# Leaving part of the scores uncopied and moving the side work of two interleaved attention loops

## Time and profile before

| | |
|---|---|
| median of 3 runs | 2729.12 us (2728.18 to 2730.86) |
| the profiled execution, its own time | 2727.77 us |
| its span | 2726.0 us |
| busy share of the span: PE, DVE, ACT, POOL | 85%, 92%, 94%, 47% |
| mean granted clock of PE | 0.979 |
| DMA | 140.84 MB, mean 52 GB/s |

### The profile page before, as it was taken

The page is one execution under the profiler, slowest core; times in us unless marked ns, Lnnn a source line. Parts: engine busy times, 40 slices in busy tenths (PEclk is TensorE's granted clock), DMA queues, the critical chain, the costliest instruction groups (busy, mean ns, idle before and its releaser), DMA issues. The chain is left out here.

```text
span 2726.0 us, 39855 instructions
## 1 busy us (share of the span) xinstructions
PE 2310.4 (85%) x12453; PEld 1084.6 (40%) x12672; DVE 2501.0 (92%) x3626; ACT 2558.9 (94%) x4763; POOL 1279.9 (47%) x1891
## 2 busy tenths in 40 slices
PE   5788888877777777777778899999999999999998
PEld 2244444433433433443342334343433434333434
DVE  5899999999999999999988999999999999999995
ACT  4899999999999999999998999999999999999994
POOL 0146566654554554554552244444344444434444
PEclk8799999999999999999999999999999999999999
DMA  7511212133211111111111111111011111111110
GB/s 212 124 55 50 82 52 72 49 93 87 64 35 43 33 35 40 38 35 35 51 33 41 49 43 35 41 45 46 29 47 44 36 39 45 43 31 47 44 30 16
DMA packets 190938, 140.84 MB, mean 52 GB/s; under 512 B 92163, under 2 KB 177669, under 8 KB 190726
## 3 DMA queue, kind: packets, MB, share of 16 engines
q1 hardware_dynamic: 190406, 137.69, 18.4%
q10 hardware_dynamic: 320, 0.59, 0.1%
HBM read 92.04 MB, written 41.94 MB: 49 GB/s over the span
## 5 line engine op out<-in xcount | busy, mean ns | idle before, releaser
L1059 DVE TENSOR_REDUCE nmax<-score 128x1 f32<-128x1024 f32 x1024 | 1196.7, 1212 | 105.7 <-PE score L823 98.8
L1032 DVE TENSOR_SCALAR_CACHE_REDUCE big<-score 128x1024 f32<-128x1024 f32 x1024 | 1194.7, 1217 | 48.2 <-PE score L761 45.5
L1264 ACT ACTIVATE big<-big,nmax 128x1024 f32<-128x1024 f32 x1024 | 1168.1, 1143 | 36.8 <-DVE big L1032 33.1
L1306 ACT ACTIVATE score<-score,nmax 128x1024 f32<-128x1024 f32 x1024 | 1119.8, 1100 | 45.7 <-DVE nmax L1059 44.5
L823 PE MATMUL score<-big,shared 128*128 128x512 bf16 x1956 | 619.7, 397 | 271.3 <-ACT score L1306 236.4
L761 PE MATMUL score<-shared 128*128 128x512 bf16 x1921 | 534.6, 382 | 57.5 <-DVE big L1032 40.3
L742 PE MATMUL bank_g<-big,qw 128*32 128x512 f32 x4096 | 492.6, 599 | 1.0 <-ACT qcol L1291 1.0
L823 PEld LDWEIGHTS score<-big,shared 128*128 128x128 bf16 x2048 | 130.2, 98 | 566.1 <-ACT score L1306 474.0
L761 PEld LDWEIGHTS score<-shared 128*128 128x128 bf16 x2048 | 165.3, 98 | 429.1 <-DVE big L1032 253.9
L717 PE MATMUL bank_f<-norms,w_fc_sb 128*128 128x128 f32 x2048 | 297.1, 278 | 45.5 <-ACT hid L1228 44.5
L717 PEld LDWEIGHTS bank_f<-norms,w_fc_sb 128*128 128x128 f32 x2048 | 278.5, 192 | 114.0 <-ACT hid L1228 75.3
(11 more groups left out here) (147 smaller groups left out, 1747.5 us busy)
## 6 DMA issues: line engine op xcount, KB each, us to landing
shared<-q_parts SPq DMA_DIRECT2D x256, 64.0 KB, 2.4
shared<-kb_parts SPq DMA_DIRECT2D x256, 64.0 KB, 2.2
shared<-vb_parts SPq DMA_DIRECT2D x256, 64.0 KB, 2.2
big<-k_parts SPq DMA_DIRECT2D x48, 192.0 KB, 5.1
big<-k_parts SPq DMA_DIRECT2D x24, 256.0 KB, 7.9
kb_parts<-pieces SPq DMA_DIRECT2D x96, 64.0 KB, 1.6
vb_parts<-pieces SPq DMA_DIRECT2D x96, 64.0 KB, 1.6
shared<-in_x SPq DMA_DIRECT2D x32, 128.0 KB, 2.3
```

Source lines behind the costliest of these rows:

```text
L1032: v.tensor_scalar(row_chunk(c), score_b(turn, c)[:, :], -1.0, INF, ALU.mult, ALU.min, accum_out=nmax[:, par, c // NCH, c % NCH:c % NCH + 1 ...
L1059: v.tensor_reduce(nmax[:, par, c // NCH, c % NCH:c % NCH + 1], score_a(turn, c)[:, :], AX.X, ALU.max, negate=True).then_inc(max_a, 1)
L1264: a.activation(row_chunk(c), row_chunk(c), ACT.Exp, bias=nmax[:, par, c // NCH, c % NCH:c % NCH + 1], scale=-1.0, accum_out=esum[:, par, c ...
L1306: a.activation(s[:, :], s[:, :], ACT.Exp, bias=nmax[:, par, c // NCH, c % NCH:c % NCH + 1], accum_out=esum[:, par, c // NCH, c % NCH:c % N ...
```

## The change

Three things are changed together.

1. In the second attention the slots in `STAGED` (21 of 32) keep the copy. In the other 11 (0, 4, 5, 7, 13, 14, 15, 26, 29, 30, 31) DVE does a reduction, as in the first attention, and ACT takes the exponential from PSUM into SBUF. For these the bank is free when the exponential is done.
2. The slots of the side work of the second attention: up projections, relu, down projections, y, the first list of `PROD_AT`, the copy of the product (slot 17 to 16), the copy of the transposed input (24 to 27), and DVE's statistics and mean (24, 25 to 27, 28).
3. In the first attention the slot numbers become a table. `BESIDE` has the old numbers and is used for iterations 0 to 10 and from 31 on; `ALONE` has new ones for iterations 11 to 30. The copy of q is split between slots 19 and 30 there.

```
+BESIDE = dict(turn_opt=9, out=[10, 11], turn_x2=12, kv=[13, 14, 15, 16], q=[18, 20],
+              turn_x1=17, up=[18, 19, 20, 21, 22, 23, 24, 25], down=[26, 26, 27, 27, 28, 29, 30, 30],
+              fac=1, take_opt=7, take_x2=10, take_x1=15, take_k=15, take_v=15,
+              take_q=[20, 20], relu=[19, 23], take_y=29,
+              rec=4, add=11, stats_x1=12, mean_x1=13, stats_x2=6, mean_x2=7)
+ALONE = dict(turn_opt=7, out=[8, 9], turn_x2=10, kv=[12, 13, 15, 15], q=[17, 19],
+             turn_x1=18, up=[19, 21, 21, 21, 23, 23, 24, 24], down=[26, 26, 27, 28, 29, 30, 31, 31],
+             fac=0, take_opt=5, take_x2=9, take_x1=17, take_k=14, take_v=14,
+             take_q=[19, 30], relu=[20, 23], take_y=30,
+             rec=3, add=9, stats_x1=14, mean_x1=15, stats_x2=1, mean_x2=5)
+UP_B = [0, 0, 1, 1, 3, 5, 5, 5]
+DOWN_B = [14, 16, 17, 17, 18, 18, 20, 21]
+RELU_B, TAKE_Y_B, KEEP_B = [0, 5], 20, 16
+STAGED = [1, 2, 3, 6, 8, 9, 10, 11, 12, 16, 17, 18, 19, 20, 21, 22, 23, 24, 25, 27, 28]
+TURN_B, COLUMNS_B = 24, 27
-PROD_AT = [7, 7, 10, 10, 13, 13, 16, 16], [22, 22, 25, 25, 28, 28, 31, 31]
+PROD_AT = [6, 6, 9, 9, 12, 12, 15, 15], [22, 22, 25, 25, 28, 28, 31, 31]
...
+        def plan(it):
+            return ALONE if N_STEPS <= it < T - 1 else BESIDE
...
-                need(pe, max_b, CPT * i + c - NBUF + 1)
+                need(pe, max_b if (c - NBUF) % CPT in STAGED else exp_b, CPT * i + c - NBUF + 1)
...
-                v.tensor_scalar(row_chunk(c), score_b(turn, c)[:, :], -1.0, INF, ALU.mult, ALU.min,
-                                accum_out=nmax[:, par, c // NCH, c % NCH:c % NCH + 1]).then_inc(max_b, 1)
+                if c in STAGED:
+                    v.tensor_scalar(row_chunk(c), score_b(turn, c)[:, :], -1.0, INF, ALU.mult, ALU.min,
+                                    accum_out=nmax[:, par, c // NCH, c % NCH:c % NCH + 1]).then_inc(max_b, 1)
+                else:
+                    v.tensor_reduce(nmax[:, par, c // NCH, c % NCH:c % NCH + 1], score_b(turn, c)[:, :],
+                                    AX.X, ALU.max, negate=True).then_inc(max_b, 1)
...
-                        if c == 24:
+                        if c == 27:
                             ffn_stats_of(T + i1, (quad + 3) % 4, x3_ready, i1 + 1)
-                        if c == 25:
+                        if c == 28:
                             ffn_mean(T + i1)
...
-                a.activation(row_chunk(c), row_chunk(c), ACT.Exp, bias=nmax[:, par, c // NCH, c % NCH:c % NCH + 1], scale=-1.0,
+                staged = c in STAGED
+                a.activation(row_chunk(c), row_chunk(c) if staged else score_b(turn, c)[:, :], ACT.Exp,
+                             bias=nmax[:, par, c // NCH, c % NCH:c % NCH + 1], scale=-1.0 if staged else 1.0,
                              accum_out=esum[:, par, c // NCH, c % NCH:c % NCH + 1]).then_inc(exp_b, 1)
```

More of the change, by code:

```diff
@@ L841, in phase_a @@
                             transpose2(bank_f, opt).then_inc(opt_tr, 1)
[L842 to L849, removed]
+                        for k in range(KC):
+                            if c == at["out"][k]:
+                                if k == 0:
+                                    pe.wait_ge(opt_T, i1 + 1)
+                                mm(bank_f[:, D:2 * D], optT[:, k, :], w_out_sb[:, k, :], start=(k == 0), stop=False)
+                                if k == KC - 1:
+                                    mm(bank_f[:, D:2 * D], ones[:, :], bias[:, D:2 * D], start=False, stop=True).then_inc(oproj, 1)
+                        if c == at["turn_x1"]:
                             ffn_transpose(i1, xn)
                         for f in range(FF // P):
-                            if c == UP_A[f]:
+                            if c == at["up"][f]:
                                 ffn_up(i1, f)
                         for f in range(FF // P):
-                            if c == DOWN_A[f]:
+                            if c == at["down"][f]:
                                 ffn_down(i1, f)
@@ L1039, in head_maxima, with out_stats @@
                     row_min(i, par, 1)
-            def out_stats(i3, r, c):
-                if c == 6:
+            def out_stats(i3, r, c, at):
+                if c == at["stats_x2"]:
                     dve.wait_ge(ffn_out, i3 + 1)
                     v.bn_stats(st[:, 1, :], xout[:, r, :]).then_inc(qkv_stats, 1)
-                if c == 7:
+                if c == at["mean_x2"]:
                     stand_alone(dve, (qkv_stats, i3 + 1), (qkv_xn, i3))
@@ L1067, in phase_a @@
                             v.tensor_tensor(nrow[:, :], nmax[:, r1, :, 0], nmax[:, r1, :, 1], ALU.min).then_inc(att_min, 1)
-                        if c == 4:
+                        if c == at["rec"]:
                             dve.wait_ge(att_sum, 2 * i1 + 2)
                             v.reciprocal(rec[:, :], tot[:, :]).then_inc(att_rec, 1)
-                        if c == 11:
+                        if c == at["add"]:
                             dve.wait_ge(oproj, i1 + 1)
@@ L1285, in project_b @@
                     a.activation(kvf[:, 0:D], bank_q[:, 0:D], ACT.Copy, scale=temp_sb[:, bass.ds(i3, 1)])
+                if c == at["take_v"]:
                     a.activation(kvf[:, D:2 * D], bank_q[:, D:2 * D], ACT.Copy).then_inc(qkv_kvf, 1)
[L1287 to L1290, removed]
+                for m in range(KC):
+                    if c == at["take_q"][m]:
+                        if m == 0:
+                            act.wait_ge(qkv_q, i3 + 1)
+                            need(act, qb_stored[r], 8 * (i3 - r))
                         last = a.activation(attention_q(i3, r)[:, m * P:(m + 1) * P], bank_q[:, m * P:(m + 1) * P],
                                             ACT.Identity, bias=bqb_col[:, m:m + 1])
-                    last.then_inc(qkv_qf, 1)
+                        if m == KC - 1:
+                            last.then_inc(qkv_qf, 1)
             def phase_a(it, turn, _):
@@ L1343, in phase_b @@
                     if left_over(it) is not None:
-                        project_b(left_over(it), 1 - par, c)
-                    if i1 is not None and c == PROD_AT[0][-1] + 1:
+                        project_b(left_over(it), 1 - par, c, BESIDE)
+                    if i1 is not None and c == KEEP_B:
                         keep_product(i1)
-                    if i2 is not None and c == TURN_B:
+                    if i2 is not None and c == COLUMNS_B:
                         ffn_columns(T + i2)
                     if i3 is not None:
-                        if c == UP_B[4] - 3:
+                        if c == RELU_B[0]:
                             ffn_act(T + i3, 0)
-                        if c == UP_B[7] - 1:
+                        if c == RELU_B[1]:
                             ffn_act(T + i3, 1)
-                        if c == DOWN_B[7] - 1:
+                        if c == TAKE_Y_B:
                             ffn_take(T + i3, 1 - par)
```

49 lines of the change are left out of this document (24 added, 25 removed).

## The result

The changed kernel takes 2656.93 us (median of 4 runs, 2654.64 to 2661.87) against 2728.65 for the kernel before on the same chips: a ratio of 0.9738, 95% interval 0.9721 to 0.9755. The forecast was 2669 us, between 2648 and 2702. The profiled execution is the slowest of the four, 2661.87 us with a span of 2660.1; it is 65.9 us under the profiled execution of before (2727.77), where the prediction had 60.

A forecast was written before the change was run, and what follows sets the result against it. No engine is idle in bulk (ACT 94%, DVE 92%, PE 85%), so tile length in each attention was taken as the bound. -26 - 38 - 1 = -65, 5 given back: -60, so 2669 us, range 2648 to 2702.

The forecast's parts named there:

- The first attention, -26: Iterations 11 to 30: tile from 40.38 to 39.1 us, 0.3 for PE's clock included; 1.3 x 20 = -26 us.
- The walk: One tile stepped through slot by slot with measured times: 38.75 us in the first attention, 38.2 in the second.
- The second attention, -38: Tile from 39.71 to 38.4 us, against ACT's own sum of 38.0; 1.3 x 29 = -38 us.
- The uncopied slots, 0.47 a tile: Second attention: ACT saves 0.043 us at each of 11 slots, 0.47 us a tile.
- the prediction's 1100: Second attention: assumed 1100 ns for an exponential from PSUM into SBUF, against 1143 from SBUF to SBUF.
- The statistics' wait: Second attention: DVE's statistics at slot 27 instead of 24 no longer wait for POOL, 0.3 us a tile on average.
- PE's waits: Second attention: PE's waits for ACT's exponentials stay under 1 us a tile; 3 or more would show the slower case.
- SP's later stores: First attention: SP's k and v stores and queued q loads start up to 10 us later, at no cost.
- Rival (a): Second attention: exponentials from PSUM still take 1143, so 15 us less is gained: 2684 us; chance 0.14.
- (b): Second attention stays bound by the chain DVE, PE, ACT; only POOL's wait goes (9 us): 2694 us; chance 0.16.
- (c): First attention gains nothing, as PE's half clock hits slots with new work or x1 is late: 2690 us; chance 0.10.
- Rival (d): Second attention: late releases at uncopied slots leave PE standing, products behind the score; tile 42.0, 2777 us; chance 0.06.

The follow-up runs named there:

- e9: The filled kernel: the changed kernel plus two more 128x512 matmuls behind the score in slots 2 to 6 of iterations 11 to 30; 2653.29 us.
- e10: Changed kernel with all 32 second-attention slots copied, first product list back at 7, 10, 13, 16 and product's copy at 17; 2663.49 us.
- e3: Changed kernel with all 32 slots of the second attention copied again, both new orders kept; 2660.87 us.
- e6: Changed kernel with the second attention's DVE statistics back at slots 24 and 25 and the transposed input's copy at 24; 2656.79 us.
- e12: Changed kernel, all slots copied, second attention's side work in old slots except first products at 6, 9, 12, 15 and product's copy at 16; 2687.99 us.
- e11: Changed kernel, all slots copied, second attention's side work in old slots except statistics at 27, 28 and transposed input's copy at 27; 2682.96 us.
- e8: Changed kernel with its 11 uncopied slots moved to 0, 3, 6, 9, 12, 19, 22, 25, 28, 30, 31; 2789.76 us.
- e4: Changed kernel with the second attention's side work back in its old slots, the 11 uncopied slots kept; 2749.37 us.

## Why the prediction was right, point by point

- **The first attention, -26.** Measured -23.2. The walk gave 38.75 for an undisturbed tile, the filled kernel has 38.90; the 0.3 kept for the clock was 0.31 (39.21 - 38.90). A walk with pace and release times from rows was good to 0.15 us in 39.
- **The second attention, -38.** Measured -39.3; 38.36 a tile, the walk had 38.2 and the forecast 38.4. The whole came out better than its terms: the gain of the uncopied slots was put too high and that of the projections' slots was not put down by itself, and that the two misses cancel is in part luck. ACT's own sum of 38.0 is missed by 0.4. With copies it is reached: e10 takes 38.44, the sum for 32 copies was 38.5.
- **The uncopied slots, 0.47 a tile.** This is the mis-sized term: e3 gives 0.22, some 6 us instead of 14. The price of one exponential was right. By the starts in the traces of the changed kernel and of e3, the step to the next exponential is 1.09 against 1.13 at slots 4, 26, 29 and 30, 0.04 saved at each. The number of slots was wrong: the prediction multiplied by eleven, though only seven of them (0, 4, 5, 26, 29, 30, 31) lie where ACT has a backlog. These save 0.26 a tile. At 7, 13, 14 and 15 DVE sets the pace, and they save 0.03 together. And as ACT now catches up with DVE, the copied slots from 6 to 12 go at DVE's 1.145 instead of ACT's 1.13 and give 0.07 back. The sum came out since it was checked against a walk, and since the projections' new slots brought 0.71 that the text had counted only inside the walk.
- **The row of an exponential is a poor price.** By the rows the saving would be 33 ns (1145 less 1112). But the copied form has 1143 before and 1260 in e10, where from the third tile on ACT has a backlog in every slot, and in the middle of e10's second attention its starts are still 1.13 apart. The step between starts is the price. By it an exponential takes 1.09 from PSUM whether it writes PSUM (first attention, rows of 1105) or SBUF (rows of 1112), so the prediction's 1100 was a fair stand-in.

```profile
L1287 ACT ACTIVATE big<-big,nmax 128x1024 f32<-128x1024 f32 x1024 | 1185.5, 1260 | 14.1 <-DVE big L1050 14.0
```

Of the two rules of the Trainium skill weighed there, the one of "VectorE: DVE Perf Modes", section on the TRN2 errata, gives by its cycles an estimate of 43 ns for the source operand; the trace agrees, with 0.04 us from start to start. The one of "ScalarE: Activation LUTs", section "Step-by-step: what each stage is for", that writing PSUM is the faster, does not show in the steps here; the rows differ by 7 ns.

- **The statistics' wait.** The wait went, as forecast. That the later slots did it was only half right: e6 and e12 show that the product's copy, a slot sooner, removes nearly all of it as well. Its size was read too low: 15.2 us in 29 tiles is 0.52 a tile at DVE and not 0.3, and e11 against the kernel before has 0.56.
- **PE's waits.** The walk had scores 1, 2 and 8 next to ACT's releases without loss; the trace has two waits a tile and 1.0 us. "Under 1 us" was at its edge.
- **SP's later stores** cost nothing that shows: tiles of 38.90 throughout in e9.
- **Rival (a)** came to about half of its size: 0.25 of the 0.47 is missing, though not for its reason, since the saving from PSUM is there. **(b)** does not hold: ACT has no wait left, though its pace is DVE's from slot 6 to 15. **(c)**: the half clock did move, into slots 1 to 8, but cost as much as before, 0.3 a tile.
- **Rival (d)**, slower, is not what this change did, but it is a real mechanism of this kernel: e8 has it at 42.54 a tile and 2789.76 us, where the prediction's price for it was 42.0 and 2777; e4 has it with the old order. What kept it out is the rule that no slot with products has an uncopied slot three before it.

The profiled execution fits the sum better than the median does (-65.9 and -71.7, forecast -60). The spans of the four runs go from 2652.8 at a mean clock of 0.982 to 2660.1 at 0.976. That the half clock falls into the first attention more or less often from run to run would explain it, and the small spread of e9 speaks for it; only one of the four has a trace, so it isn't shown.

## What to carry to other kernels

When a buffer's release moves from an early engine to a late one, the cost is not set by how many slots do so but by what stands in the feeding engine's queue right behind the waiting slot: against copies in all slots, eleven such slots changed the tile by -0.2 us or by +4.0, by their places alone. Price a cheaper instruction only in the slots in which its engine has a backlog, by the step from start to start and not by the length of its row, and set against it the order that it forces on the rest. And where PE's clock falls in or behind light stretches, as here, a handful of useless matmuls there can pay.

## What the hardware showed that I had not expected

Two extra matmuls of 128x512 in each of five slots keep PE's clock full through 778 us, at no cost to the tile (38.90 against 38.91 in the undisturbed tiles of the changed kernel): PE had 0.66 us of each such slot to spare (1.09 less a score's 0.43). And in the changed kernel eight of the 20 tiles are 0.6 to 0.9 us longer than the undisturbed ones, although PE is busy only 80% of that stretch. In the one of them looked at, with the clock of 0.56, the row of a score (two matmuls) is 1.03 us long instead of 0.60, and it lies in the ring of three banks, which by the prediction's sum has no play.
